# Perceiver, window attention and ternary feed-forward on one core: the instructions of all five engines in another order

## The reference

```
h = layernorm(x)
for l in 0..3:
    q, k, v = rmsnorm(h, n1) @ Wqkv.T + bqkv       # 16 heads of 16; rope on q and k
    h = h + softmax(causal(q k / 4)) v @ Wo.T + bo
    q = rmsnorm(h, n2) @ Wq_c.T ; k, v = ctx @ Wkv_c.T
    h = h + softmax(masked(q k / 4)) v @ Wo_c.T    # key j in (id - 128, id], id = token id, 0..63
    m = rmsnorm(h, n3)
    h = h + (silu(m @ Wg.T) * (m @ Wu.T)) @ Wd.T   # 1024 inner channels
x = x + rmsnorm(h, nf)
y = layernorm(x)                                   # window attention over the 16 tokens before
y = y + sum_w sigmoid(q k_w / 4) v_w @ wo.T
x = x + layernorm(y) * gamma + beta
x = x + ternary_mlp(layernorm(x))                  # weights rounded to -1, 0, 1; tokens to 8-bit steps
```

## Time and profile before

| what | us |
|---|---|
| median of 3 runs | 584.85 (584.66 to 585.15) |
| the profiled execution, span of the core | 584.8 |
| PE busy | 528.3 |
| DVE busy | 356.2 |
| ACT busy | 282.2 |
| POOL busy | 116.2 |
| mean granted PE clock, share of full | 0.982 |

### The profile page before, as it was taken

One profiled execution on the slowest core, in us unless ns is written; L12 is line 12 of the kernel. 1 busy time (PEld: TensorE's weight loads), 2 busy tenths in 40 slices (PEclk: granted clock), 3 DMA queues, 4 the chain that ended last, 5 costly groups with the idle time before them and its releaser, 6 DMA issues.

```text
span 584.8 us, 15276 instructions
## 1 busy us (share of the span) xinstructions
PE 528.3 (90%) x6585; PEld 409.0 (70%) x6586; DVE 356.2 (61%) x669; ACT 282.2 (48%) x509; POOL 116.2 (20%) x125
## 2 busy tenths in 40 slices
PE   4988898999998988999998989999989989899765
PEld 2666665988676656988766649987766669887514
DVE  5977356566564655665745474573755546752796
ACT  1165654623346456433445636243574666326542
POOL 5241200022332100021622000021621001621100
PEclk9999999999999999999999989999999989999977
DMA  8300080010500100200501200203101100000001
GB/s 324 151 2 2 3 322 4 14 61 1 217 38 3 39 36 3 73 0 2 216 2 39 75 1 1 73 1 142 76 7 31 67 2 1 1 0 2 2 2 40
DMA packets 4682, 30.38 MB, mean 52 GB/s; under 512 B 1153, under 2 KB 1665, under 8 KB 2818
## 3 DMA queue, kind: packets, MB, share of 16 engines
q1 hardware_dynamic: 4610, 29.35, 13.5%
HBM read 28.82 MB, written 0.52 MB: 50 GB/s over the span
## 4 chain that ended last, share of the span: by engine, by line
PE 73%; DVE 13%; ACT 9%; issue 2%; POOL 1%; DVEq 0%; ACTq 0%; POOLq 0%
PE psD L345 15%; PE QD L688 13%; PE psD L701 10%; PE QD L442 7%; DVE AQ L1904 5%; PE QD L482 5%; ACT PTR L1331 4%; PE psD L339 3%; PE psD L502 3%; PE psD L688 2%; PE psD L523 2%; PE psD L509 2%; PE QD L475 2%; PE psD L383 2%; DVE MX L1901 2%
## 5 line engine op out<-in xcount | busy, mean ns | idle before, releaser
L1331 ACT ACTIVATE PTR<-QD 128x2048 f32<-128x2048 f32 x40 | 74.9, 1873 | 56.4 <-PE QD L482 47.5
L1904 DVE TENSOR_REDUCE AQ<-QD 128x8 f32<-128x2048 f32 (+1 forms) x24 | 55.0, 2291 | 27.7 <-PE QD L442 27.5
L688 PE MATMUL QD<-HH,WFH 128*128 128x256 f32 x224 | 69.1, 309 | 1.7 <-DVE WFL L2008 1.7
L2605 POOL TENSOR_TENSOR rstd<-ms,mhalf 128x2 f32<-128x2 f32 x26 | 19.2, 737 | 250.0 <-DVE ms L1827 246.8
L688 PE MATMUL QD<-HL,WFH 128*128 128x256 f32 x224 | 63.3, 283 | 0.0
L688 PE MATMUL QD<-HH,WFL 128*128 128x256 f32 x224 | 63.3, 283 | 0.0
L1901 DVE TENSOR_REDUCE MX<-QD 128x16 f32<-128x2048 f32 x16 | 36.7, 2293 | 39.6 <-PE QD L442 39.6
L2008 DVE TENSOR_TENSOR WFL<-WC,WFH 128x512 fp32r<-128x512 f32 x64 | 46.5, 757 | 20.0 <-ACT WFH L1377 19.4
L701 PE MATMUL psD<-WC,HID 128*128 128x256 f32 x256 | 58.5, 382 | 0.0
L345 PE MATMUL psD<-WAB,hT 128*128 128x256 f32 (+1 forms) x152 | 53.2, 488 | 0.9 <-DVE hT L1842 0.9
L701 PEld LDWEIGHTS psD<-WC,HID 128*128 128x128 f32 x256 | 47.6, 190 | 7.2 <-issue 1.0
(11 more groups left out here) (186 smaller groups left out, 992.2 us busy)
## 6 DMA issues: line engine op xcount, KB each, us to landing
WC<-in_wc SPq DMA_DIRECT2D x4, 3072.0 KB, 10.2
WAB<-in_wa SPq DMA_DIRECT2D x4, 1024.0 KB, 6.4
WAB<-in_wb SPq DMA_DIRECT2D x4, 1024.0 KB, 4.8
WF<-in_wf SPq DMA_DIRECT2D x1, 3072.0 KB, 11.3
bias<-in_bias SPq DMA_DIRECT2D x4, 512.0 KB, 5.7
WAB<-in_wt SPq DMA_DIRECT2D x1, 1024.0 KB, 7.4
X<-in_x SPq DMA_DIRECT2D x2, 256.0 KB, 2.7
out_x<-X SPq DMA_DIRECT2D x4, 128.0 KB, 2.4
```

The costliest lines, as they stand in the source:

```text
L688: mm = pe.matmul(S[:, w * L:(w + 1) * L], wp[:, m, :], hp[:, k, :], start=(k == 0 and j == 0), stop=(k == KT - 1 and j == 2))
L1331: nc.scalar.activation(PTR[:, r % 2, :], QD[:, :], ACT.Exp, scale=SCALE if r < SELF_ROUNDS else 1.0).then_inc(t_exp, 1)
L1904: v = dve.tensor_reduce(QKR[b][:, t, 0, h, MAXROW].rearrange("p (s r) -> p r s", r=SG_H), QD[:, :].rearrange("p (r s n) -> p r s n", r=4, ...
```

## The change

The calls in the blocks of tensor, scalar, vector and gpsimd are put in another order. The sync block, so every transfer's issue and place, is as before. Each engine issues the same instructions as before, no operation, operand, tile or buffer is changed, and none is added or removed. The waits inside the helpers follow the new order (the counts that `next_bank` and `free_for` work out). The diff, cut to the stretches where something of consequence moves; the left-out parts are of the same kind, and indentation is shortened:

```diff
@@ -832,19 +832,19 @@
 def layer(l, further):
  outputs_T(l, 2)
  scores(l, 4)
- maxima_T(l, 3)
  out_T(l, 0, "oT0", 2)
  rotated_T(l, 1, 1, 1)
+ maxima_T(l, 3)
  cross_kT(l, 0)
  scores_T(l, 3)
  out_proj(l, 0, "wo0", Wo, "oT0")
  scores(l, 5)
+ pv(l, 3)
  maxima_T(l, 4)
- pv(l, 3)
- outputs_T(l, 3)
- norm_T(l, 1, 0)
  scores_T(l, 4)
  maxima_T(l, 5)
+ norm_T(l, 1, 0)
+ outputs_T(l, 3)
  cross_q(l, 0)
  scores_T(l, 5)
  cross_kv(l, 0)
@@ -855,11 +855,11 @@
  outputs_T(l, 5)
  scores(l, 7)
  out_T(l, 1, "oT1", 5)
- cross_kv(l, 1)
  maxima_T(l, 6)
  out_proj(l, 1, "wo1", Wo, "oT1")
  scores_T(l, 6)
  maxima_T(l, 7)
+ cross_kv(l, 1)
  cross_kT(l, 1)
  norm_T(l, 1, 1)
...
  gate_up(l, 1, 6)
- rotated_T(l + 1, 0, 0, 0)
+ rotated_T(l + 1, 0, 1, 1)
  gate_up(l, 1, 7)
  scores(l + 1, 0)
  down(l, 1, range(0, 4))
- rotated_T(l + 1, 0, 1, 0)
+ scores(l + 1, 1)
  maxima_T(l + 1, 0)
- rotated_T(l + 1, 0, 1, 1)
- scores(l + 1, 1)
  down(l, 1, range(4, FT))
+ maxima_T(l + 1, 1)
  scores_T(l + 1, 0)
- maxima_T(l + 1, 1)
  values(l + 1, 0)
  norm_T(l + 1, 0, 1)
  scores(l + 1, 2)
  queries_keys(l + 1, 1, 0)
  queries_keys(l + 1, 1, 1)
+ maxima_T(l + 1, 2)
  scores_T(l + 1, 1)
- pv(l + 1, 0)
- maxima_T(l + 1, 2)
  values(l + 1, 1)
  rotated_T(l + 1, 1, 0, 0)
+ pv(l + 1, 0)
  scores_T(l + 1, 2)
- outputs_T(l + 1, 0)
  rotated_T(l + 1, 1, 0, 1)
  rotated_T(l + 1, 1, 1, 0)
+ outputs_T(l + 1, 0)
  pv(l + 1, 1)
  scores(l + 1, 3)
  outputs_T(l + 1, 1)
...
@@ -950,10 +950,10 @@
 causal_strips()
 queries_keys(0, 0, 0)
 queries_keys(0, 0, 1)
+values(0, 0)
+rotated_T(0, 0, 0, 0)
+rotated_T(0, 0, 0, 1)
 norm_T(0, 0, 1)
-values(0, 0)
-rotated_T(0, 0, 0, 1)
-rotated_T(0, 0, 0, 0)
 scores(0, 0)
 rotated_T(0, 0, 1, 0)
 queries_keys(0, 1, 0)
...
 scores_T(0, 0)
-maxima_T(0, 1)
+maxima_T(0, 2)
 rotated_T(0, 1, 0, 1)
+scores_T(0, 1)
+pv(0, 0)
 rotated_T(0, 1, 0, 0)
-scores_T(0, 1)
-maxima_T(0, 2)
-rotated_T(0, 1, 1, 0)
-pv(0, 0)
 scores_T(0, 2)
 outputs_T(0, 0)
 pv(0, 1)
+rotated_T(0, 1, 1, 0)
 scores(0, 3)
 outputs_T(0, 1)
 pv(0, 2)
-rotated_T(0, 1, 1, 1)
+key_mask_strips(0)
 outputs_T(0, 2)
 scores(0, 4)
+rotated_T(0, 1, 1, 1)
 maxima_T(0, 3)
+cross_kT(0, 0)
 out_T(0, 0, "oT0", 2)
 scores_T(0, 3)
+out_proj(0, 0, "wo0", Wo, "oT0")
+query_mask_strips(0)
+scores(0, 5)
+query_mask_strips(3)
 maxima_T(0, 4)
-out_proj(0, 0, "wo0", Wo, "oT0")
-scores(0, 5)
-key_mask_strips(0)
 cross_kv(0, 0)
 pv(0, 3)
 scores_T(0, 4)
-maxima_T(0, 5)
-cross_kT(0, 0)
 outputs_T(0, 3)
 norm_T(0, 1, 0)
+query_mask_strips(1)
+maxima_T(0, 5)
+query_mask_strips(2)
 scores_T(0, 5)
-query_mask_strips(0)
-query_mask_strips(1)
 cross_kT(0, 1)
 cross_q(0, 0)
-query_mask_strips(2)
+pv(0, 4)
 key_mask_strips(1)
 key_mask_strips(2)
-query_mask_strips(3)
-pv(0, 4)
 scores(0, 6)
 outputs_T(0, 4)
 pv(0, 5)
+key_mask_strips(3)
 outputs_T(0, 5)
 scores(0, 7)
 out_T(0, 1, "oT1", 5)
-key_mask_strips(3)
 maxima_T(0, 6)
 out_proj(0, 1, "wo1", Wo, "oT1")
 scores_T(0, 6)
...
+ rotated_T(1, 0, 1, 1)
  down(0, 1, range(0, 4))
- rotated_T(1, 0, 1, 0)
  maxima_T(1, 0)
- rotated_T(1, 0, 1, 1)
  scores(1, 1)
  down(0, 1, range(4, FT))
  scores_T(1, 0)
  norm_T(1, 0, 1)
  values(1, 0)
  scores(1, 2)
+ queries_keys(1, 1, 0)
  maxima_T(1, 1)
- queries_keys(1, 1, 0)
+ pv(1, 0)
  scores_T(1, 1)
+ maxima_T(1, 2)
  queries_keys(1, 1, 1)
- maxima_T(1, 2)
- pv(1, 0)
- scores_T(1, 2)
- values(1, 1)
- rotated_T(1, 1, 0, 1)
  rotated_T(1, 1, 0, 0)
  outputs_T(1, 0)
+ scores_T(1, 2)
+ rotated_T(1, 1, 0, 1)
+ values(1, 1)
  pv(1, 1)
  scores(1, 3)
  outputs_T(1, 1)
...
@@ -1149,43 +1149,43 @@
  out_proj(NL - 1, 0, "cwo0", Woc, "coT0")
  scores_T(NL - 1, 8)
  maxima_T(NL - 1, 9)
+ band_strips(0)
  norm_T(NL - 1, 2, 0)
  scores_T(NL - 1, 9)
  pv(NL - 1, 8)
  gate_up(NL - 1, 0, 0)
...
- gate_up(NL - 1, 0, 7)
  down(NL - 1, 0, range(0, 4))
  norm_T(NL - 1, 2, 1)
+ gate_up(NL - 1, 0, 7)
  down(NL - 1, 0, range(4, FT))
  gate_up(NL - 1, 1, 0)
  gate_up(NL - 1, 1, 1)
  gate_up(NL - 1, 1, 2)
  gate_up(NL - 1, 1, 3)
  gate_up(NL - 1, 1, 4)
+ down(NL - 1, 1, range(0, 4))
  gate_up(NL - 1, 1, 5)
- down(NL - 1, 1, range(0, 4))
+ window_T(0)
  gate_up(NL - 1, 1, 6)
  gate_up(NL - 1, 1, 7)
- window_T(0)
  down(NL - 1, 1, range(4, FT))
+ window_qk(0, 0)
  window_qk(0, 1)
- window_qk(0, 0)
  window_middle_v(0)
  window_scores(0, 0)
  window_v(0)
@@ -1193,13 +1193,13 @@
  window_scores(0, 1)
  window_qk(1, 0)
  window_qk(1, 1)
- window_middle_v(1)
  window_pv(0, 0)
  window_pv(0, 1)
  window_scores(1, 0)
...
@@ -1477,12 +1477,13 @@
  copy_oT(l, 0, "oT0")
  query_max_strips(l, 3)
  self_strips(l, 1, 1, 1)
+ split_high(l, 0)
  exp(l, 3)
  squares(l, 1, 0)
+ key_strips(l, 0)
  query_max_strips(l, 4)
- key_strips(l, 0)
+ split_high(l, 1)
  strip_outputs(l, 3)
- split_high(l, 0)
  exp(l, 4)
  query_max_strips(l, 5)
  query_strips(l, 0, 0)
...
 self_strips(0, 1, 1, 1)
-copy_oT(0, 0, "oT0")
-query_max_strips(0, 3)
 exp(0, 3)
+key_strips(0, 0)
+query_mask_strips(0)
 squares(0, 1, 0)
-split_high(0, 1)
 query_max_strips(0, 4)
-key_mask_strips(0)
 strip_outputs(0, 3)
+query_mask_strips(3)
 exp(0, 4)
 query_max_strips(0, 5)
-key_strips(0, 0)
+query_mask_strips(2)
+query_mask_strips(1)
 exp(0, 5)
 key_strips(0, 1)
-query_mask_strips(0)
-query_mask_strips(1)
 query_strips(0, 0, 0)
-query_mask_strips(2)
+split_high(0, 1)
 query_strips(0, 0, 1)
-query_mask_strips(3)
+strip_outputs(0, 4)
 key_mask_strips(1)
 key_mask_strips(2)
-strip_outputs(0, 4)
 strip_outputs(0, 5)
+key_mask_strips(3)
 copy_oT(0, 1, "oT1")
...
  strip_outputs(NL - 1, 2)
  sum_abs(0)
  sum_abs(1)
+ sum_abs(2)
+ sum_abs(3)
+ query_max_strips(NL - 1, 3)
  self_strips(NL - 1, 1, 1, 1)
- sum_abs(2)
  copy_oT(NL - 1, 0, "oT0")
- query_max_strips(NL - 1, 3)
+ exp(NL - 1, 3)
  key_strips(NL - 1, 0)
- exp(NL - 1, 3)
...
  divide(l, 0)
  maxima(l, 3)
  divide(l, 1)
  divide(l, 2)
  maxima(l, 4)
  residual(l, 0, "wo0")
+ maxima(l, 5)
  mean_square(l, 1, 0)
- maxima(l, 5)
  normalise(l, 1, 0)
  weigh_T(l, 1, 0)
+ cross_kv(l, 0)
  divide(l, 3)
- cross_kv(l, 0)
  maxima(l, 6)
- split_low(l, 0)
  divide(l, 4)
  divide(l, 5)
  maxima(l, 7)
- cross_kv(l, 1)
  query_max_strips(l, 6)
  residual(l, 1, "wo1")
+ split_low(l, 0)
  mean_square(l, 1, 1)
  query_max_strips(l, 7)
  normalise(l, 1, 1)
+ split_low(l, 1)
+ cross_kv(l, 1)
  weigh_T(l, 1, 1)
  maxima(l, 8)
  divide(l, 6)
  divide(l, 7)
- split_low(l, 1)
  if further:
   all_blocks(l, 0)
  maxima(l, 9)
...
@@ -2304,148 +2304,148 @@
 dve.wait_ge(pads_set, 1)
 layernorm_stats(0, 0, X0)
 centre(0)
+mean_square(0, 0, 0)
 small_constants()
-mean_square(0, 0, 0)
 weigh_T(0, 0, 0)
 layernorm_stats(1, 1, X0)
 mean_square(0, 0, 1)
 first_scale(0)
-centre(1)
-layernorm_apply(0, 0, X0, X, lambda v: v.then_inc(x_kept[0], 1))
 biased_qk(0, 0, 0)
+key_sines(0, 0)
 cosines(0, 0, 0)
-key_sines(0, 0)
 biased_qk(0, 0, 1)
 add_sines(0, 0, 0)
+centre(1)
+cosines(0, 0, 1)
+key_sines(0, 1)
+biased_v(0, 0)
+add_sines(0, 0, 1)
 weigh_T(0, 0, 1)
-biased_v(0, 0)
-key_sines(0, 1)
-cosines(0, 0, 1)
-add_sines(0, 0, 1)
 maxima(0, 0)
+layernorm_apply(0, 0, X0, X, lambda v: v.then_inc(x_kept[0], 1))
 first_scale(1)
+maxima(0, 1)
 biased_qk(0, 1, 0)
+biased_v(0, 1)
+maxima(0, 2)
 cosines(0, 1, 0)
-maxima(0, 1)
 add_sines(0, 1, 0)
-maxima(0, 2)
 biased_qk(0, 1, 1)
-biased_v(0, 1)
 cosines(0, 1, 1)
+blocks_to_go()
 add_sines(0, 1, 1)
-blocks_to_go()
 divide(0, 0)
+masks()
 maxima(0, 3)
-layernorm_apply(1, 1, X0, X, lambda v: v.then_inc(x_kept[1], 1))
 divide(0, 1)
 divide(0, 2)
 maxima(0, 4)
-masks()
 residual(0, 0, "wo0")
 maxima(0, 5)
+mean_square(0, 1, 0)
 cross_kv(0, 0)
-mean_square(0, 1, 0)
+layernorm_apply(1, 1, X0, X, lambda v: v.then_inc(x_kept[1], 1))
 normalise(0, 1, 0)
 dve.wait_ge(nb_set, 1)
 nb = dve.value_load(NB[0:1, 0:1], min_val=0, max_val=NBLK)
 def rest(further):
...
  split_low(NL - 1, 3)
+ split_low(NL - 1, 4)
+ hidden(NL - 1, 0, 0)
  divide(NL - 1, 8)
- hidden(NL - 1, 0, 0)
- split_low(NL - 1, 4)
- hidden(NL - 1, 0, 1)
+ split_low(NL - 1, 5)
  hidden(NL - 1, 0, 2)
- split_low(NL - 1, 5)
+ divide(NL - 1, 9)
+ hidden(NL - 1, 0, 3)
  split_low(NL - 1, 6)
- hidden(NL - 1, 0, 3)
- divide(NL - 1, 9)
  hidden(NL - 1, 0, 4)
  split_low(NL - 1, 7)
  if further:
   all_blocks(NL - 1, 1)
+ means()
+ split_low(NL - 1, 8)
+ residual(NL - 1, 1, "cwo1")
  hidden(NL - 1, 0, 5)
- split_low(NL - 1, 8)
- means()
- residual(NL - 1, 1, "cwo1")
+ mean_square(NL - 1, 2, 1)
+ normalise(NL - 1, 2, 1)
+ hidden(NL - 1, 0, 6)
+ weigh_T(NL - 1, 2, 1)
+ tokens_high(NL - 1, 1)
+ hidden(NL - 1, 0, 7)
  split_low(NL - 1, 9)
- mean_square(NL - 1, 2, 1)
- hidden(NL - 1, 0, 6)
- normalise(NL - 1, 2, 1)
- weigh_T(NL - 1, 2, 1)
...
- tokens_high(NL - 1, 1)
+ tokens_low(NL - 1, 1)
  split_low(NL - 1, 10)
- tokens_low(NL - 1, 1)
  residual(NL - 1, 0, "y0")
  split_low(NL - 1, 11)
+ split_low(NL - 1, 12)
+ hidden(NL - 1, 1, 0)
  mean_square(NL, 0, 0)
- hidden(NL - 1, 1, 0)
- split_low(NL - 1, 12)
+ add_layers(0)
  hidden(NL - 1, 1, 1)
+ layernorm_stats(2, 0, X0)
+ hidden(NL - 1, 1, 2)
  split_low(NL - 1, 13)
```

(53 more changed lines are left out.)

364 lines of the change are left out of this document (184 added, 180 removed).

## The result

The changed kernel takes 590.65 us (median of 9 runs, 588.37 to 591.88), the kernel before in the same comparison 585.15 (median of 9, 582.99 to 588.29). The ratio is 1.0075, 95% interval 1.0049 to 1.0102: slower by 0.75%, some 4.4 us. The forecast was 584.2, in a range of 581.0 to 587.2, which doesn't hold it.

A forecast was written before the change was run, and what follows sets the result against it. PE, busy 528.3 of 584.8 us, bounds the MLPs, PE or QD's chain the attention, DVE's chain the tail. Terms -1.1 - 1.0 + 0.2 - 0.8 - 0.05 + 0.35 + 1.5 + 0.3 = -0.6 give 584.2, range 581.0 to 587.2.

The forecast's parts named there:

- Layer 0's head: Start of layer 0: moved layernorm_apply, centre(1) and norm_T delay the first maxima by 0.8 us, bounds 0 and +1.4.
- Masks: Layer 0: masks (2.44 us) ahead of maxima(3), where DVE idles 1.96, costs +0.4 us, bounds 0 and +0.5.
- To S6: Layer 0, maxima(5) to S6: strips made earlier shorten 12.06 us to 9.4, -2.6, possibly 0.
- Rival B: Layer 0's strips give nothing back, as PE queues behind a psD bank awaiting divide; 586.8 us, chance 0.19.
- Start of layer 1: Layer 1's attention: T1's wait of 1.43 us for maxima(1) goes but for 0.4; -1.0, bounds -1.3 and 0.
- MLPs at nothing: MLP stretches: PE has no idle time, 40.00 of 40 us, so moves there can't win, only lose.
- Starts of layers 2 and 3: Self attention starts bound by PE's work; moved rotations and causal cost nothing, -0.3 to +1.0 us if cover is thin.
- End of layer 3's MLP: The 1.75 us stall goes, but scale_ternary(0) and (1) hold DVE for +1.0 and +1.1; +0.35, bounds -1.75 and +1.5.
- Start of the tail: scale_ternary(2) on POOL holds add_layers and window_k, +1.8 less 0.3: +1.5 us, bounds -0.05 and +2.5.
- Last stage: End of kernel: round_hidden(2) and ternary ahead of the chain, +0.6, less PE queue, -0.3: +0.3 us, bounds -0.4 and +1.0.
- Rival A: POOL's holds of DVE at layer 3's MLP end and in the tail don't bite; 580.5 us, chance 0.25.
- Rival C: PE's clock: the new order brings falls at two more places or spares two; 586.8 or 581.6 us, chance 0.13.

The follow-up runs named there:

- e6: Kernel before with the new order of layer 0 alone, but masks() behind maxima(4) and key_mask_strips(0) next to key_mask_strips(3); ratio 0.9991 (0.9965 to 1.0017).
- e1: Kernel before with the new order from the start to round 3 of layer 1's self attention, old order behind; ratio 0.9997 (0.9966 to 1.0028).
- e4: Changed kernel with POOL's scale_ternary(2) moved behind add_beta(1); ratio 1.0050 (1.0022 to 1.0078) against the kernel before.
- e11: Changed kernel with the old order in the second half of the MLPs of layers 0, 1 and 2; 1.0077 (1.0040 to 1.0113) against the kernel before.
- e5: Changed kernel with its last stage, behind the window attention, in the old order; ratio 1.0101 (1.0062 to 1.0140) against the kernel before.
- e10: Changed kernel with DVE's biased_v(2, 1) moved right behind cosines(2, 1, 1), ahead of add_sines; ratio 1.0082 (1.0051 to 1.0114) against the kernel before.
- e7: Kernel before with the new order only in layer 1's and layer 2's MLP and rounds 0 to 3 behind each; ratio 1.0075 (1.0045 to 1.0105).
- e2: Kernel before with the new order from round 3 of layer 1 to the end of layer 3's cross attention; ratio 1.0061 (1.0030 to 1.0092).
- f3: Kernel before with POOL's scale_ternary(2) moved from behind rsqrt(4, 0, 0) to right behind rsqrt(4, 0, 1); ratio 1.0059 (1.0030 to 1.0089), +3.5 us.
- f2: Kernel before with only its last stage, behind the window attention, in the new order; ratio 1.0041 (1.0010 to 1.0071), +2.4 us.

## Why the prediction was wrong

The step that failed is the price of the losses. The prediction counted holds of DVE by POOL at three places, all in layer 3's MLP and the tail, and took none for more than its own length; it did not look for them in layer 0 and in the other MLPs, and it put at nothing the bank ring in the starts of layers 2 and 3, and the clock. Its own sign of being wrong throughout, a shift of more than 1 us where it had nothing, came at the start of layer 2 (+1.50). Part by part:

- *Layer 0's head, +0.8*: measured +0.70, but executions with the old head had its first maxima between 0.26 and 1.72 later than the profiled one. Not to be told from nothing.
- *Masks, +0.4*: **failed**, +1.72 of maxima(3), of which e6 keeps 0.38 with `masks` back in its place, and then +1.42 of exp(3). I set masks' 2.44 against an idle of 1.96 as if they would start at the same time. But `blocks_to_go` was moved ahead of `add_sines` too, beside POOL's work, and held to 2.6 us more than in before; `add_sines` ended only at 40.8, so the idle time I counted on was used up, and `masks` was held for 0.8 more. Without these 3.4 it would have ended about 43.3 (an estimate: `divide(0, 0)` at before's place, 0.7 later for the head, and masks' 2.44), beside the 43.12 at which S3 ended. The +1.42 of exp(3) is the fall of the clock: from maxima(3) to exp(3) the profiles of this order take 9.0 with it (four: after, e1, e4, e11) and 7.57 without (e5 and e10), at the same wait of 1.5 before S4. The old order had a wait of 1.48 in this stretch too, before T3, and no fall in the six profiles that have it.
- *To S6, -2.6*: right, -3.10, with 9.13 for the forecast 9.4. Rival B didn't happen.
- *Start of layer 1, -1.0*: right, -1.00. That the `mean_square` of 1.28 was itself a hold, by `causal`, I had not seen; the order took it away all the same, which in part is luck.
- *MLPs at nothing*: **failed**. I wrote that a change inside an MLP can only lose, and priced that at 0. Layer 0 lost 1.1 and layer 2 1.2, layer 1 nothing. The rows showed PE without idle, not how early DVE was; in layer 0 an `add_sines` took 1.66 beside POOL's `add_bo`.
- *Rounds 4 and 5, +0.1 a layer*: +0.20 and +0.21, the right mechanism. *Rounds 6 and 7, -0.4 a layer*: -0.13 each; T6 gained less than the copy.
- *Starts of layers 2 and 3 at 0 (to +1.0)*: **failed**, +1.50 and +0.65, by the bank ring and a held `add_sines`. "Behind PE's products" wasn't worked out with the ring of four banks. e7 shows this and the MLPs to be the middle's loss.
- *Layer 3's attention, -0.05*: +0.17.
- *End of layer 3's MLP, +0.35*: -2.57 on the table, of which 1.6 is the clock fall from 472 to 480 that the profile of before has and no other. Without one (e1, e2, e7 and f3 for the old order, after and e4 for the new) the way from exp(3, 9) to residual y1 is 45.6 to 45.7 and 44.7, so -1.0. The holds of `normalise` and `split_low` came as forecast, and PE's work covered them. The gain is against a hold that is not certain: in f2, with the old order there, the same `mean_square` was let through between POOL's two instructions, PE had no wait of 1.75, and the way took 43.8. POOL and DVE of f2:

```profile
501.91 2.48 POOL L2942 TENSOR_SCALAR WF<-WF,rw 128x2048 f32<-128x2048 f32 x1
504.33 2.72 POOL L2935 MEMSET AQ<- 128x1536 f32 x2
...
502.68 1.73 DVE L2000 TENSOR_SCALAR ms<-ss 128x2 f32<-128x2 f32 x1
```

- *Start of the tail, +1.5*: mechanism right, **size wrong**: the hold is 1.71 as forecast (1.8), but with the wait of 2.27 comes a clock fall. f3 measures +3.5 for this one call.
- *Last stage, +0.3*: **size wrong**, f2 measures +2.4 (0.6 to 4.2) and the profiles +1.2. I counted instructions and not ACT's `ternary` ahead of `scale_hidden`, 1.14 of ACT on a chain; that this call is the cause is read from the waits, no run moves it alone.

The forecast saw most of the places and gave the two large gains their right size; of the losses it priced the visible wait only. The sum of its terms, -0.6, was the difference of 4.5 of gains and 3.9 of losses, and a range of 6 us around such a sum was too narrow. Rival A fell: the holds bite. Rival C, the clock, was taken as luck, with a mean of nothing. In this change falls came with the new waits in two of three places: behind S4's 1.5 in four of six profiles, behind the tail's 2.27 in all six that have it, behind the 1.51 of `rotated_T` in none of five.

The hold agrees with the rule that the prediction drew from the Trainium skill ("SBUF — State Buffer", the two separate sides): 2.59, 2.32 and 1.61 for 0.88, 0.62 and 0.61, each time with POOL's operation 0.05 to 0.07 ahead and DVE's end 0.4 to 0.7 behind POOL's. The Trainium skill limits the rule there to VectorE instructions in a two-port mode or with two inputs in SBUF, which the prediction left out. The traces agree with this as well: over all profiles 88 maxima, which read PSUM, started while a POOL instruction ran, and all took 2.28 or 2.29.

What stays open: what decides at a given wait whether the clock falls; how much of e4's and e10's gains in place reaches the end, which the times can't resolve; and the size of the last stage's loss, for which e5 and f2 nearly disagree.

## What to carry to other kernels

Look at what the cross-engine neighbour of a chain does in the microsecond after it releases the chain: a long POOL operation right behind the rsqrt that DVE waits for cost 3.5 us here, and standing two calls further on it holds nothing. Small instructions are held as well: one on a single element took 1.02 for 0.15. A new wait on PE may cost more than its length, by a fall of the clock: 1.4 to 1.6 us each here, in all six profiles with the wait in the tail, and not always elsewhere. In an order with a ring of banks, count four uses back at each moved call; that caught the change once and my own experiments twice. And measure a stretch between landmarks that the change doesn't move.

## What the runs showed of the hardware

- Within one kernel the longest runs are those with a lower mean granted clock. In the first set the kernel before took 581.3 to 583.2 at a clock of 0.988 to 0.993, and 587.3 to 588.8 at 0.983 to 0.985. In between the clock doesn't order the runs: 585.1 at 0.982, 586.1 at 0.991.
- A fall costs 1.4 to 1.6 us in the attention stretches (the same stretch of the same order with and without one), and where it comes differs between executions: in the profiles with the old order at these places, before has falls at 344 and 472 us, e7 at 100, f3 at neither.
- The length of one wait doesn't decide alone whether a fall comes. PE's `norm_T` behind round 8 waited 1.53 or 1.54 in layers 0, 1 and 2 of all seventeen profiles, and 11 of these 51 waits have a fall beside them.
- A held DVE instruction of 0.15 us can take 4.39, through two POOL instructions in a row; in f2 the same one took 1.73 and ended between the two.
- The first maxima come 0.26 to 1.72 us later in executions whose head has the same order as before's.
